# A two-layer attention and state-space kernel: ScalarE's table phases merged, loads reordered, B and C rows in four column tiles

## The chip, the cores and the metric

The kernel runs on one core of one Trainium2 chip. The metric is device time in microseconds of one launch; before the change the median of three runs is 849.88 us (849.84 to 852.37). A profile of one execution stands beside these runs. The engines are TensorE (PE; PEld are its weight loads), VectorE (DVE), ScalarE (ACT), GpSimd (POOL) and SyncE (SP), whose queue issues all DMAs here.

## The reference

Sixteen images of 16 x 16 positions and 64 channels go through two layers, all in float32.

- The first is attention over a 2 x 2 max-pooled image: `theta`, `phi` and `g` are projections of x, softmax of theta times phi weighs g, and the result, projected back, is added to x times `sigma`.
- The second reads each image in four directions (as it is, mirrored in width, in height, in both). Each direction is RMS-normalised and goes through a state-space mixer with 128 inner channels and 16 states: an input projection gives `hs` and `gate`; `hs` goes through a causal convolution of four taps and SiLU and becomes u; projections of u give a step width dt (through softplus) and, for every position, 16 values B and 16 values C. The recurrence is

```
state_n = exp(dt * A_n) * state_n + dt * B_n * u
y       = sum over n of state_n * C_n,  then  (y + u * D) * silu(gate),  projected back
```

The residual is added, RMS-normalised, the four directions are turned back and averaged, and a layer norm ends it.

## The kernel before

**Tiling.** 128 inner channels lie on the partitions, and the four directions of 256 positions stand side by side in 1024 columns. For each image and each of the 16 states n there is one scan of 128 x 1024 on VectorE (`scan`, L1129), with a decay factor and an input; where a direction begins, the step is overwritten with a huge number so that the decay is zero. The scanned state is multiplied with C's row (`product`), and TensorE adds the products of all states up in `ps_y` with an identity matmul (`sum_state`, L580).

**Three kinds of state.** The string `KIND = "ACCPACCCCPACPPCC"` says for each n who does what:

- C (1, 2, 5, 6, 7, 8, 11, 14, 15): ScalarE writes the decay into a PSUM tile `ps_x[n % 2]` (`ps_decay`, L798), POOL multiplies `du` with B's row (`scan_input`, L1000), VectorE scans inside `ps_x` and multiplies with C itself (L1146).
- P (3, 9, 12, 13): the same, but the scan goes to SBUF and POOL multiplies with C (L1008).
- A (0, 4, 10): ScalarE makes the input from transposed tiles, eight scalings each (`act_input`, L825), TensorE turns it into `ps_x` (`turn_input`, L564), the decay goes to SBUF (`sb_decay`, L806, called the shared decay in what follows), VectorE scans, POOL multiplies.

There are two tiles `ps_x`, so the decay of n may be written only when state n - 2 has let go of its tile: for kind C after its product, for the others after its scan (`x_free_wait`, L280). Decay 8 thus waits for product 6, decay 9 for product 7.

**Rows of B and C.** For an image, `bc_proj` (L491) projects u to 32 rows, ScalarE copies them to `bc_rows`, SP stores them to DRAM (`store_bc`), and loads them back row by row, each spread over 128 partitions (512 KB a load; `load_b`, L334, `load_c`, L341). B goes through a ring of four buffers that POOL's inputs release; C n waits for product n - 4. `bt_turn` (L545) transposes the rows for states of kind A.

**Order.** Every engine runs a list written out by hand: a prologue for the first two images, then `steps(b, done, coming, later)` for each image b, then a finish. In one step the engines work on four images: the scans of b, the end of the image before (`done`: gating, projection, norms), the preparation of the next (`coming`: norm, convolution, SiLU, softplus, rows), and the attention of the one after (`later`). Nothing is reordered at run time: an instruction that waits holds up what is behind it on its engine, and a load that waits holds up the loads behind it in SP's queue.

**ScalarE's tables.** SiLU, softplus and Exp/Ln belong to three table sets; `silu_table` (L772), `exp_table` (L775) and `softplus` (L784) load the set they need. In a step before the change the preparation of the next image has three phases, with decays of image b around them:

```
ps_decay 3 | pad, hid_inverse | silu_table, conv_silu half 0, exp_table | ps_decay 5
ps_decay 6 | silu_table, conv_silu half 1, gate_silu, exp_table | ps_decay 7
ps_decay 8 | softplus (own table), exp_table | ps_decay 9
```

The first half of the step projection (`step_proj`, L483) needs the gate copied out of its PSUM tile; softplus needs both halves. POOL's `scan_weight` (L991) follows softplus.

## Time and profile before

| | |
|---|---|
| median of the runs | 849.88 us (849.84 to 852.37) |
| profiled execution | 855.12 us |
| span of its instructions | 852.9 us |
| granted TensorE clock, mean | 0.988 |
| table loads on ScalarE | 94 (46 and 31 and 16, and one ahead) |
| DMA | 248.98 MB, mean 292 GB/s |

The span runs from the first to the last instruction of the profile; the execution's own time has a little around it. A row of a timeline gives the start in us from the span's start, the duration, engine, line, operation, what it writes and reads, and in brackets the engine's idle time before it and what ended it; like instructions that follow each other are merged ("x2"), so the row's duration is that of both. Instructions of an engine may overlap by a little, and matmuls in float32 appear as two records each. A row of the page's part 5 has the busy time of its group and the mean duration in ns.

### The profile page before, as it was taken

The page shows a single profiled execution, that of the slowest core. Times are in us where ns is not written, and L with a number is a line of the kernel's source. Part 1 is how long each engine was busy: PE and PEld are TensorE (multiplying, and loading weights), DVE is VectorE, ACT ScalarE, POOL GpSimd, SP SyncE. Part 2 cuts the span into 40 slices and gives each one's busy share as a digit, 9 for nine tenths or more (in the row PEclk, how much of TensorE's full clock was granted, in tenths as well). Part 3 has the DMA queues.
Part 4 walks back from the last instruction along what each step waited for, and adds up shares of the span by engine and source line. Part 5 has one row for each costly group of instructions (what it writes and reads, how often), then busy time and mean ns, then how long its engine had stood idle before and what let it go on. Part 6 is the DMA issues. An engine that isn't in the chain of part 4 may idle for free.

```text
span 852.9 us, 10113 instructions
## 1 busy us (share of the span) xinstructions
PE 792.3 (93%) x2592; PEld 386.7 (45%) x2592; DVE 787.9 (92%) x537; ACT 732.0 (86%) x1310; POOL 785.0 (92%) x363
## 2 busy tenths in 40 slices
PE   8489999999999999999999999999999999999795
PEld 6234444454444444444444544544454444444332
DVE  2299999999999999999999999999999999999992
ACT  5898989899898998989899998989999898987431
POOL 1399999999999999999999999999999999999980
PEclk9899999999999999999999999999999999999998
DMA  1679888889998989999898899988899988989870
GB/s 46 230 265 328 303 302 295 312 301 314 329 312 304 324 277 316 313 326 305 305 325 304 317 315 326 302 314 320 293 327 295 333 289 320 305 311 309 298 259 6
DMA packets 74472, 248.98 MB, mean 292 GB/s; under 512 B 12592, under 2 KB 13872, under 8 KB 74416
## 3 DMA queue, kind: packets, MB, share of 16 engines
q1 hardware_dynamic: 74416, 248.35, 85.0%
q8 instruction: 21, 0.34, 0.2%
q14 instruction: 35, 0.29, 0.1%
HBM read 245.17 MB, written 3.15 MB: 291 GB/s over the span
## 4 chain that ended last, share of the span: by engine, by line
POOL 40%; DMA 34%; issue 12%; PE 4%; DVE 3%; ACT 3%; SPq 3%; POOLq 0%; DVEq 0%; ACTq 0%
DMA b_all<-bc_dram 29%; POOL state L1011 19%; POOL inp L1005 18%; DMA c_all<-bc_dram 5%; POOL du L995 2%; SPq L344 2%; DVE state L1136 1%; PE ps_y L586 1%; DVE ps_x L1143 1%; ACT ps_x L804 1%; DVE state L1150 1%; PE ps_x L421 0%; ACT L786 0%; ACT L776 0%; ACT step L789 0%
## 5 line engine op out<-in xcount | busy, mean ns | idle before, releaser
L1005 POOL TENSOR_TENSOR inp<-du,b_all 128x1024 f32<-128x1024 f32 x208 | 487.7, 2364 | 14.5 <-issue 7.8
L586 PE MATMUL ps_y<-state,packed 128*128 128x512 f32 x1024 | 475.9, 600 | 17.6 <-POOL state L1011 16.9
L1143 DVE TENSOR_TENSOR_SCAN ps_x<-ps_x,inp 128x1024 f32<-128x1024 f32 x144 | 325.8, 2283 | 6.2 <-ACT ps_x L804 4.9
L586 PEld LDWEIGHTS ps_y<-state,packed 128*128 128x128 f32 x1024 | 188.2, 191 | 230.1 <-issue 183.5
L804 ACT ACTIVATE ps_x<-step,a_neg 128x1024 f32<-128x1024 f32 x208 | 231.0, 1111 | 48.5 <-DVE state L1150 21.8
L1011 POOL TENSOR_TENSOR state<-state,c_all 128x1024 f32<-128x1024 f32 x112 | 263.7, 2361 | 8.0 <-DVE state L1136 6.2
L1150 DVE TENSOR_TENSOR state<-ps_x,c_all 128x1024 f32<-128x1024 f32 x144 | 172.9, 1214 | 7.9 <-issue 3.9
L1143 DVE TENSOR_TENSOR_SCAN state<-ps_x,inp 128x1024 f32<-128x1024 f32 x64 | 145.7, 2279 | 3.1 <-issue 2.7
L1136 DVE TENSOR_TENSOR_SCAN state<-decay,ps_x 128x1024 f32<-128x1024 f32 x48 | 109.2, 2275 | 14.2 <-PE ps_x L572 12.8
L834 ACT ACTIVATE scaled<-dut,bt 128x128 f32<-128x128 f32 x384 | 117.1, 388 | 0.5
L475 PE MATMUL ps_w<-xpad,w_conv 128*128 128x512 f32 x128 | 60.4, 594 | 1.2 <-ACT xpad L762 1.2
L995 POOL TENSOR_TENSOR du<-step,u 128x1024 f32<-128x1024 f32 x16 | 37.9, 2370 | 24.0 <-ACT step L789 24.0
L776 ACT ACT_TABLE_LOAD x46 | 59.0, 1283 | 0.8
L572 PE MATMUL ps_x<-packed,scaled 128*128 128x128 f32 x384 | 51.4, 278 | 7.4 <-DVE state L1150 4.1
L572 PEld LDWEIGHTS ps_x<-packed,scaled 128*128 128x128 f32 x384 | 43.4, 142 | 28.6 <-issue 24.7
L811 ACT ACTIVATE decay<-step,a_neg 128x1024 f32<-128x1024 f32 x48 | 54.7, 1139 | 0.0
L773 ACT ACT_TABLE_LOAD x31 | 39.8, 1283 | 0.5
L475 PEld LDWEIGHTS ps_w<-xpad,w_conv 128*128 128x128 f32 x128 | 22.4, 188 | 33.9 <-issue 31.8
L577 PE MATMUL ps_y<-u,diag_d 128*128 128x512 f32 x64 | 34.2, 617 | 0.0
L488 PE MATMUL ps_w<-u,w_step 128*128 128x512 f32 x64 | 30.2, 594 | 0.0
L823 ACT ACTIVATE dut<-ps_w 128x512 f32<-128x512 f32 x32 | 19.1, 597 | 8.0 <-PE ps_w L561 7.2
L769 ACT ACTIVATE u<-ps_w,packed 128x512 f32<-128x512 f32 x32 | 21.9, 688 | 3.9 <-PE ps_w L475 3.6
(124 smaller groups left out, 642.4 us busy)
## 6 DMA issues: line engine op xcount, KB each, us to landing
c_all<-bc_dram SPq DMA_DIRECT2D x256, 512.0 KB, 6.2
b_all<-bc_dram SPq DMA_DIRECT2D x208, 512.0 KB, 6.6
bc_dram<-bc_rows SPq DMA_DIRECT2D x32, 64.0 KB, 2.2
xa<-in_x_t SPq DMA_DIRECT2D x16, 64.0 KB, 7.3
out<-ofin SPq DMA_DIRECT2D x16, 64.0 KB, 4.3
packed<-in_packed SPq DMA_DIRECT2D x1, 635.0 KB, 4.2
packed<-in_packed SPq DMA_DIRECT2D x1, 129.0 KB, 2.6
w_qkv<-in_w_qkv SPq DMA_DIRECT2D x1, 64.0 KB, 2.0
```

The source lines that it names most:

```text
L475: last = mm(ps_w[:, HALF * half:HALF * (half + 1)], w_conv[:, 2 * half + tap2, :], moved, start=(tap2 == 0), stop=(tap2 == 1))
L572: last = nc.tensor.transpose(ps_x[n % 2][:, 128 * k:128 * (k + 1)], scaled[i % A_RING][:, k, :], ident)
L586: last = mm(ps_y[:, HALF * half:HALF * (half + 1)], ident, state[n % H_RING][:, HALF * half:HALF * (half + 1)], start=(n == 0), stop=(n == ...
L776: act.preload_act_table_set(EXP_LN)
L804: f(ps_x[n % 2][:, :], step[b.buf][:, :], ACT.Exp, scale=a_neg[:, n:n + 1]).then_inc(ps_decay_done, 1)
L834: last = f(scaled[i % A_RING][:, k, :], dut[b.buf][:, k, :], ACT.Copy, scale=bt[b.buf][:, at, row:row + 1])
L995: tt(du[j.buf][:, :], step[j.buf][:, :], u[j.buf][:, :], ALU.mult).then_inc(du_done, 1)
L1005: tt(inp[i % IN_RING][:, :], du[b.buf][:, :], b_all[i % B_RING][:, :], ALU.mult).then_inc(pool_inputs, 1)
L1011: tt(state[n % H_RING][:, :], state[n % H_RING][:, :], c_all[n % C_RING][:, :], ALU.mult).then_inc(pool_products, 1)
L1136: v.tensor_tensor_scan(held, decay[i % D_RING][:, :], x, 0.0, ALU.mult, ALU.add).then_inc(scans, 1)
L1143: v.tensor_tensor_scan(held if KIND[n] == "P" else x, x, inp[i % IN_RING][:, :], 0.0, ALU.mult, ALU.add).then_inc(scans, 1)
L1150: v.tensor_tensor(state[n % H_RING][:, :], ps_x[n % 2][:, :], c_all[n % C_RING][:, :], ALU.mult).then_inc(dve_products, 1)
```

## The change

ScalarE: the second SiLU half, gate's SiLU and softplus follow each other between `ps_decay` 8 and 9, with one Exp load at their end; the first SiLU half moves behind `ps_decay` 6; `sb_decay` 10 moves ahead of `pad`, `sb_decay` 0 of the next image between decays 11 and 12; the residual of an image ends the step before. `bc_proj` makes its 32 rows for each direction (256 columns) in a column tile of its own, so that `bc_rows` is 128 x 256, is transposed in two pieces and stored in four. `hid_residual` is one matmul. SP loads B 6 and C 2 and 3 in the image before, and C 5 and 6 ahead of B 11; the next image's C 0 now stands ahead of its B 1. TensorE, VectorE and POOL have new orders; POOL does product 3 ahead of input 7. Warm-up multiplies are moved in the prologue and added in the finish. In the softmax the copy of `gw` follows the exponentials. The diff, cut to its core:

```diff
 SP, steps
-                load_b(b, 6)
-                load_c(b, 2)
-                load_c(b, 3)
-                load_c(b, 4)
                 load_b(b, 7)
                 load_b(b, 8)
                 load_b(b, 9)
-                load_b(b, 11)
+                load_c(b, 4)
                 load_c(b, 5)
                 load_c(b, 6)
+                load_b(b, 11)
                 load_b(b, 12)
...
                 load_c(b, 15)
                 if coming:
+                    load_c(coming, 0)
+                    load_b(coming, 1)
                     load_b(coming, 2)
+                    load_c(coming, 1)
                     load_b(coming, 3)
-                    load_c(coming, 0)
-                    load_c(coming, 1)
                     load_b(coming, 5)
+                    load_c(coming, 2)
+                    load_b(coming, 6)
+                    load_c(coming, 3)
 TensorE
-                for half in range(2):
-                    last = mm(bank[2 * N * half:2 * N * (half + 1), 0:HALF], w("w_bc"),
-                              u[j.buf][:, HALF * half:HALF * (half + 1)], start=True, stop=True)
+                for d in range(DIRS):
+                    last = mm(bank[2 * N * d:2 * N * (d + 1), 0:L], w("w_bc"), u[j.buf][:, L * d:L * (d + 1)],
+                              start=True, stop=True)
...
-                for rows in range(2):
-                    mm(w1[C * rows:C * (rows + 1), :], ident[:, C * rows:C * (rows + 1)],
-                       x2[j.num % X2_RING][:, :].unsqueeze(1).broadcast_to([128, 2, L]), start=True, stop=False)
+                mm(w1, ident, x2[j.num % X2_RING][:, :].unsqueeze(1).broadcast_to([128, 2, L]),
+                   start=True, stop=False)
 TensorE, finish
                 sum_state(j, 14)
-                hid_residual(j)
                 sum_state(j, 13)
                 sum_state(j, 15)
+                hid_residual(j)
                 hid_proj(j)
+                warm(2)
                 hid_mean(j)
+                warm(3)
                 out_mean(j)
+                warm(2)
                 out_square(j)
+                warm(2)
                 out_final(j)
 ScalarE, prologue
                 softplus(first)
                 exp_table(first)
+                softmax_exp(second)
                 bt_copy(first)
                 dut_copy(first, 0)
+                sb_decay(first, 0)
+                attn_copy(second)
                 dut_copy(first, 1)
                 act_input(first, 0)
-                sb_decay(first, 0)
+                residual(second)
                 act_input(first, 4)
 ScalarE, steps
+                ps_decay(b, 1)
                 sb_decay(b, 4)
                 if coming:
-                    residual(coming)
-                ps_decay(b, 1)
+                    rms_inverse(coming)
                 ps_decay(b, 2)
-                if coming:
-                    rms_inverse(coming)
+                ps_decay(b, 3)
                 act_input(b, 10)
                 if done:
                     hid_squares(done)
-                ps_decay(b, 3)
+                sb_decay(b, 10)
+                if done:
+                    hid_inverse(done)
                 if coming:
                     pad(coming)
-                if done:
-                    hid_inverse(done)
+                ps_decay(b, 5)
+                ps_decay(b, 6)
                 if coming:
                     silu_table(coming)
                     conv_silu(coming, 0)
                     exp_table(coming)
-                ps_decay(b, 5)
                 if done:
                     out_squares(done)
-                ps_decay(b, 6)
+                ps_decay(b, 7)
+                ps_decay(b, 8)
                 if coming:
                     silu_table(coming)
                     conv_silu(coming, 1)
                     gate_silu(coming)
-                    exp_table(coming)
-                ps_decay(b, 7)
-                sb_decay(b, 10)
-                ps_decay(b, 8)
-                if coming:
                     softplus(coming)
                     exp_table(coming)
                 ps_decay(b, 9)
                 if coming:
                     bc_copy(coming)
                     bt_copy(coming)
+                ps_decay(b, 11)
+                if coming:
                     dut_copy(coming, 0)
-                ps_decay(b, 11)
+                    sb_decay(coming, 0)
                 ps_decay(b, 12)
+                if coming:
+                    dut_copy(coming, 1)
                 if later:
                     theta_copy(later)
                 if coming:
-                    dut_copy(coming, 1)
                     act_input(coming, 0)
                 ps_decay(b, 13)
...
 POOL, steps
-                product(b, 3)
+                scan_input(b, 7)
                 scan_input(b, 8)
...
                     scan_input(coming, 6)
-                    scan_input(coming, 7)
+                    product(coming, 3)
 VectorE, steps
+                if done:
+                    product(done, 15)
                 scan(b, 0)
                 scan(b, 1)
+                if coming:
+                    rms(coming)
+                product(b, 1)
                 if done:
                     gated(done)
-                product(b, 1)
-                if coming:
-                    rms(coming)
                 scan(b, 2)
...
                 scan(b, 12)
+                scan(b, 13)
+                scan(b, 14)
+                if done:
+                    out_norm(done)
                 if later:
                     row_max(later)
-                scan(b, 13)
-                scan(b, 14)
-                if done:
-                    out_norm(done)
                 product(b, 14)
                 scan(b, 15)
-                product(b, 15)
```

## Rows read from the trace of the kernel before

**Rows 1.** The page, part 1: busy us, share of the span, instructions

```profile
PE 792.3 (93%) x2592; PEld 386.7 (45%) x2592; DVE 787.9 (92%) x537; ACT 732.0 (86%) x1310; POOL 785.0 (92%) x363
```

**Rows 2.** Timeline, DVE: start us, us; scan 10 of the first and last image

```profile
69.49 2.26 DVE L1136 TENSOR_TENSOR_SCAN state<-decay,ps_x 128x1024 f32<-128x1024 f32 x1
...
818.41 2.26 DVE L1136 TENSOR_TENSOR_SCAN state<-decay,ps_x 128x1024 f32<-128x1024 f32 x1
```

**Rows 3.** Timeline, DVE: scan 9, then scan 9 of the next image

```profile
616.10 2.29 DVE L1143 TENSOR_TENSOR_SCAN state<-ps_x,inp 128x1024 f32<-128x1024 f32 x1 [0.20 <-issue]
...
656.05 2.33 DVE L1150 TENSOR_TENSOR state<-ps_x,c_all 128x1024 f32<-128x1024 f32 x2
658.57 4.48 DVE L1143 TENSOR_TENSOR_SCAN ps_x<-ps_x,inp 128x1024 f32<-128x1024 f32 x2 [0.19 <-ACT ps_x L804]
662.96 2.33 DVE L1150 TENSOR_TENSOR state<-ps_x,c_all 128x1024 f32<-128x1024 f32 x2
665.49 2.29 DVE L1143 TENSOR_TENSOR_SCAN state<-ps_x,inp 128x1024 f32<-128x1024 f32 x1 [0.20 <-issue]
```

**Rows 4.** Timeline, ACT: the same stretch before that scan 9

```profile
654.44 0.69 ACT L769 ACTIVATE u<-ps_w,packed 128x512 f32<-128x512 f32 x1
655.03 0.65 ACT L782 ACTIVATE gate<-ps_w 128x256 f32<-128x256 f32 x2
...
658.40 1.13 ACT L811 ACTIVATE decay<-step,a_neg 128x1024 f32<-128x1024 f32 x1
659.44 1.10 ACT L804 ACTIVATE ps_x<-step,a_neg 128x1024 f32<-128x1024 f32 x1
660.56 1.28 ACT L786 ACT_TABLE_LOAD   x1
661.86 1.11 ACT L789 ACTIVATE step<-ps_w,packed 128x1024 f32<-128x1024 f32 x1
...
664.28 1.12 ACT L804 ACTIVATE ps_x<-step,a_neg 128x1024 f32<-128x1024 f32 x1
```

**Rows 5.** The page, part 5: one group of table loads

```profile
L773 ACT ACT_TABLE_LOAD x31 | 39.8, 1283 | 0.5
```

**Rows 6.** Timeline, PE: the step projection, both halves

```profile
655.79 1.88 PE L488 MATMUL ps_w<-u,w_step 128*128 128x512 f32 x4
```

**Rows 7.** Timeline, ACT: what stands ahead of the decay of scan 13

```profile
621.80 0.38 ACT L715 ACTIVATE theta<-ps_w 8x256 f32<-8x256 f32 x1
622.21 0.60 ACT L823 ACTIVATE dut<-ps_w 128x512 f32<-128x512 f32 x1
622.84 2.45 ACT L834 ACTIVATE scaled<-dut,bt 128x128 f32<-128x128 f32 x8
625.19 1.10 ACT L804 ACTIVATE ps_x<-step,a_neg 128x1024 f32<-128x1024 f32 x1
```

**Rows 8.** Timeline, DVE: the row maximum and scan 13

```profile
626.31 0.26 DVE L1118 TENSOR_REDUCE nmax<-ps_w 128x2 f32<-128x128 f32 x1
626.49 2.27 DVE L1143 TENSOR_TENSOR_SCAN state<-ps_x,inp 128x1024 f32<-128x1024 f32 x1
```

**Rows 9.** Timeline, POOL: product 12, then the next image's first input

```profile
626.46 2.35 POOL L1011 TENSOR_TENSOR state<-state,c_all 128x1024 f32<-128x1024 f32 x1 [0.20 <-DVE state L1143]
...
633.41 4.67 POOL L1005 TENSOR_TENSOR inp<-du,b_all 128x1024 f32<-128x1024 f32 x2
```

**Rows 10.** Timeline, SP's queue: a c load after product 12

```profile
628.88 0.32 SPq L344 DMA_DIRECT2D c_all<-bc_dram  x1
```

**Rows 11.** The page, part 6: DMA issues, KB each, median us to landing

```profile
b_all<-bc_dram SPq DMA_DIRECT2D x208, 512.0 KB, 6.6
```

**Rows 12.** Timeline, DVE: scan 1 of the first image

```profile
41.22 2.30 DVE L1143 TENSOR_TENSOR_SCAN ps_x<-ps_x,inp 128x1024 f32<-128x1024 f32 x1 [2.10 <-ACT ps_x L804]
```

**Rows 13.** Timeline, PE: the last image's residual multiply

```profile
834.09 1.08 PE L507 MATMUL ps_w<-x,packed 128*64 128x512 f32 x4
```

**Rows 14.** Timeline, DVE: the last image's gating

```profile
838.84 1.29 DVE L1161 TENSOR_TENSOR yg<-ps_y,gate 128x512 f32<-128x512 f32 x2 [3.25 <-PE ps_y L586]
```

More of the change, by code:

```diff
@@ L135, in build @@
         du = [sb(f"du_{q}", [I, T]) for q in range(2)]
-        bc_rows = sb("bc_rows", [128, HALF])
-        bt = [sb(f"bt_{q}", [128, HALF // 128, 4 * N]) for q in range(2)]
+        bc_rows = sb("bc_rows", [128, L])
+        bt = [sb(f"bt_{q}", [128, CHUNKS, 2 * N * DIRS]) for q in range(2)]
         dut = [sb(f"dut_{q}", [128, TURNS, I]) for q in range(2)]
@@ L357, in prologue @@
                 load_b(first, 2)
+                load_c(first, 0)
                 load_b(first, 3)
-                load_c(first, 0)
                 load_c(first, 1)
                 load_b(first, 5)
+                load_c(first, 2)
+                load_b(first, 6)
+                load_c(first, 3)
             def finish(j):
@@ L496, in bc_proj @@
                 bank = ps_w if j.num > 0 else ps_y
-                for half in range(2):
-                    last = mm(bank[2 * N * half:2 * N * (half + 1), 0:HALF], w("w_bc"),
-                              u[j.buf][:, HALF * half:HALF * (half + 1)], start=True, stop=True)
+                for d in range(DIRS):
+                    last = mm(bank[2 * N * d:2 * N * (d + 1), 0:L], w("w_bc"), u[j.buf][:, L * d:L * (d + 1)],
+                              start=True, stop=True)
                 last.then_inc(bc_mm, 1)
@@ L548, in bt_turn @@
                 if j.num == 0:
-                    pe.wait_ge(rows_zeroed, 1)
                     pe.wait_ge(step_done, 1)
-                for k in range(HALF // 128):
+                for k in range(CHUNKS):
                     last = nc.tensor.transpose(w0[:, 128 * k:128 * (k + 1)], bc_rows[:, 128 * k:128 * (k + 1)], ident)
@@ L614, in prologue @@
                 conv(first, 1)
-                attn_turn(second)
                 pe.wait_ge(weights_ready, 1)
@@ L831, in act_input @@
                 for k in range(TURNS):
-                    half, at = k // (TURNS // 2), k % (TURNS // 2)
-                    row = 2 * N * half + n
+                    at = k % CHUNKS
+                    row = 2 * N * (k // CHUNKS) + n
                     last = f(scaled[i % A_RING][:, k, :], dut[b.buf][:, k, :], ACT.Copy,
@@ L886, in prologue @@
                 pad(first)
-                softmax_exp(second)
+                state_decay()
                 silu_table(first)
@@ L1017, in prologue @@
                 scan_input(first, 1)
+                scan_input(first, 2)
                 product(first, 0)
-                scan_input(first, 2)
                 scan_input(first, 3)
@@ L1022, in prologue @@
                 scan_input(first, 6)
-                scan_input(first, 7)
+                product(first, 3)
             def finish(j):
@@ L1180, in prologue @@
                 pooling(first)
+                attn_setup()
                 row_max(first)
-                attn_setup()
+                rms(first)
+                pooling(second)
                 conv_setup()
                 setup()
-                rms(first)
-                pooling(second)
+                first_bc(first)
                 row_max(second)
-                first_bc(first)
             def finish(j):
+                product(j, 15)
                 gated(j)
@@ L1223, in steps @@
                 scan(b, 12)
-                if later:
-                    row_max(later)
                 scan(b, 13)
```

91 lines of the change are left out of this document (43 added, 48 removed).

## The prediction

> **What bounds the kernel now.** I read the busy shares first: TensorE, VectorE and POOL are each busy for 92 or 93% of the span, ScalarE for 86% [rows 1]. Such a share is a mean over prologue, images and tail, so I then followed VectorE's timeline, because its scans are a strict series: scan 9 of one image starts at 616.10 and of the next at 665.49, a period of 49.39 us [rows 3]. VectorE's 787.9 us over 16 images is 49.2 per image [rows 1]. **VectorE has next to no air in a period**, and POOL, with 785.0, only a little more. A wait that VectorE gains in each image is therefore paid in full, 15 or 16 times.
>
> The whole of it: scan 10 of the first image starts at 69.49 and of the last at 818.41, so 15 periods take 748.92 [rows 2]. Fifteen times 49.39 is 740.85; 8.07 us are lost in longer periods. The profiled execution took 855.12 and the median of the runs is 849.88, 5.24 lower, so I suppose that 2.8 of those 8.07 are left in the median run. Without them the profiled execution would take 847.05; call this the floor of the old order.
>
> In each period there is one place that the change touches and where ScalarE already ends a wait of VectorE. Product 6 ends at 658.38 and scan 9 starts at 665.49, 7.11 us later, after scans 7 and 8 and products 7 and 8; there VectorE idles 0.20 us [rows 3]. ScalarE's rows say why: the decay that scan 9 reads starts at 664.28, directly behind softplus and the load of the Exp table, and ends 0.09 before the scan [rows 4]. Nothing can be put ahead of this decay without moving scan 9.
>
> **The one large term: the merged phase.** Before, the second SiLU half and gate's SiLU ran between decays 6 and 7 with a phase of their own. Now they stand between decay 8 and softplus; the shared decay of state 10 leaves its place between decays 7 and 8. Decay 8 overwrites the PSUM tile that product 6 has read, so it starts 0.1 behind product 6 at the earliest (the hand-over in the other direction is 0.09). From there, by [rows 4] with the table load of [rows 5]: decay 8 takes 1.12 until the next starts; SiLU table 1.28; second SiLU half 0.59; gate's SiLU 0.65; softplus table 1.30; softplus and Exp table together 2.42; decay 9 with its hand-over 1.21. With the 0.1 that is 8.67 after product 6, against VectorE's 7.11: scan 9 starts **1.56 us later in every image that has a next one, 15 times: 23.4 us**. As a lower end I take 1.2, both hand-overs free and ScalarE's instructions overlapping by some 0.1 [rows 7]; a gain is excluded, since decay 8 cannot start before product 6 ends and the chain has no gap. For the upper end: softplus needs both halves of the step projection, and the first half needs the gate copied out. Two halves take 1.88 on TensorE [rows 6]; the second runs beside the gate's SiLU, the first ends 663.35 on the old clock, 0.07 before softplus could start. If both had to follow the gate, softplus would be 0.6 later: 2.2 per image.
>
> One table load less per image shortens ScalarE by 15 x 1.28 = 19 us of its 732 [rows 1, 5]. I cost this at nothing: what it shortens is the stretch from decay 3 to decay 7, and decay 7 waits for product 5 there. Into that stretch go the shared decay of state 10 (1.04, [rows 4]) and the padding ahead of decay 5; if the load's 1.28 less did not cover them, scan 5 would be late by what is left over, which I take as none.
>
> **A second, small wait.** The shared decay of state 0 moves from behind decay 15 to between decays 11 and 12. From the start of scan 9, the chain to scan 13 is then: scan 9 2.29, hand-over 0.1, decay 11 1.12, first transposed copy 0.63, the shared decay 1.04, decay 12 1.12, second copy 0.63, theta 0.41, eight scalings 2.35, decay 13 1.10, hand-over 0.09: 10.88 [rows 3, 4, 7]. VectorE's own way is 626.49 - 616.10 less 0.18 for the row maximum, which moves behind scan 14: 10.21 [rows 3, 8]. The wait is between nothing and 0.67. Where two such instructions follow each other the second starts some 0.1 early (1.13 long, 1.04 apart); with that for the decays and copies it is 0.27, which I take: 15 x 0.27 = **4.1 us**.
>
> **SP's order and the narrower rows.** Loads of B 6 and C 2 and 3 move into the image before, C 5 goes ahead of B 11, and four row stores replace two. An issue takes 0.32 [rows 10]; two more per image lie behind C 12's load, and the loads behind them wait for later products anyway. I cost that at nothing. Its cover is the new, longer period; without it, see the second rival. Earlier C loads and longer periods should end the 8.07 of loss; I take all of it as gone, ends 0 and 8.07. Four column tiles and half the transposes take only TensorE time: two tiles side by side do four records in 1.08, where one tile needs 1.88 [rows 6, 13]. The residual in one matmul is so worth some 0.14, the B and C rows between nothing and half of 1.08. TensorE waits for products between these; nothing. On VectorE, the row scaling and product 1 now precede the gating; nothing is added or removed.
>
> **Head.** Residual of the second image and the first decay now run ahead of where VectorE waited 2.10 us for decay 1 [rows 12]; softmax moves behind softplus, the first product after one more B row. I take -2.1, between nothing and -4, since the first scan itself may come earlier. **Tail.** The last gating waited 3.25 us for the sums, of which 1.08 were the residual multiply ahead of them; this now runs behind them, beside the gating: -1.1 [rows 13, 14]. Warm-up multiplies fill TensorE's waits there; as nine calls of a quarter of that width, two records each, they would cost 2.4 us at most if nothing hid them.
>
> **The sum**, on the profiled execution: 855.12 - 8.07 + 23.4 + 4.1 - 2.1 - 1.1 = 871.4 us. From the median, with its 2.8 of loss taken off, it is the same. That the forecast and this sum agree with the unprofiled time rests on the supposition that the 5.24 are such loss; if none of it goes, the time is 874 by the median, 879 by the profile.
>
> **Rivals.** *Faster: less table loading reaches the end.* If VectorE had room for the late decay 9, what stays is the floor without head and tail gains paid back: 847.05 - 3.2 = 843.9, or 846.7 with the loss kept. It decides if the merged phase fits into 7.11 us after product 6, which needs 1.56 us less on ScalarE, more than one whole load. For it speaks that ScalarE is the least busy of the four [rows 1]; against it, that scan 9 waits already. Chance 0.11. The Trainium skill (page "ScalarE: Activation LUTs", section "Rules for kernel authors") has this as a rule: group functions by table set and finish one set before switching, which speaks for the change. The same page (section "What ACT_TABLE_LOAD costs") counts a drain beside a load, 2.66 us per switch; by this an estimated 40 us of ScalarE would be saved, and the one switch that now comes between products would make scan 9 a further 1.38 us later. The load's 1283 ns agree with this trace; a drain behind it does not show, as softplus starts 0.02 behind its load [rows 4, 5].
>
> *POOL becomes the bound.* The next image's first B load now queues behind its C 0 load, and that waits for product 12. Product 12 ends at 628.81; the C issue starts 0.07 later and takes 0.32 [rows 9, 10], and a B load lands 6.6 us after its own issue [rows 11]: 635.9 with the gap between issues, where POOL wanted it at 633.41. POOL's cycle, 785.0/16 = 49.1, would be 51.6 and VectorE's 49.39 + 1.83 = 51.2: 15 x 0.4 = 6 more, 877. It decides once a landing takes over 6.3; at 8 it gives 897. Chance 0.13. Early loads and an emptier queue speak against it.
>
> **How the numbers follow.** The forecast has 0.76; its own range is 861 (1.2 per image, no second wait) to 883 (0.6 more per image, some loss kept). The range 858 to 883 holds that, most of the second rival, and leaves the faster one out. About 0.3% is what a measurement here can tell from no change, 847.3 to 852.4. The faster rival lies mostly below: 0.08 faster, 0.03 same; the rest, 0.89, slower.
>
> **What would show it.** Right: periods of about 51.2 between scans 9; ScalarE's new row group in a series SiLU load, SiLU, gate, softplus load, softplus, Exp load; VectorE's wait before scan 9 near 1.8, released by a decay; 15 table loads fewer. Wrong: no such wait, or periods near 49.4 (first rival), or POOL idle over 2 us before its first input with VectorE waiting for that input (second).

## The result and the profile after

The changed kernel takes 866.82 us (median of four runs, 865.56 to 868.55), the kernel before beside it 851.12 (849.84 to 853.27): a ratio of **1.0169, 95% interval 1.0141 to 1.0198**. It is 15.7 us slower. The forecast was 871.4 with a range of 858 to 883. The profiled execution took 868.55 with a span of 866.5 and a mean granted clock of 0.973; before it was 855.12, 852.9 and 0.988.

The page after the change, part 1 (busy us, share of the span, instructions), as [rows 1]:

```profile
PE 790.1 (91%) x2610; PEld 389.2 (45%) x2610; DVE 783.0 (90%) x537; ACT 710.2 (82%) x1295; POOL 784.8 (91%) x362
```

ScalarE has 15 instructions fewer and is busy for 21.8 us less than the 732.0 before; VectorE (787.9 before) and POOL (785.0) have nearly the work that they had. The engine that was relieved was not the one that sets the period. The timeline of VectorE after, scan 10 of the first and of the last image, as [rows 2]:

```profile
70.02 2.26 DVE L1136 TENSOR_TENSOR_SCAN state<-decay,ps_x 128x1024 f32<-128x1024 f32 x1
...
834.12 2.26 DVE L1136 TENSOR_TENSOR_SCAN state<-decay,ps_x 128x1024 f32<-128x1024 f32 x1
```

So the head takes 70.02 us (69.49 before), the 15 periods 764.10 (748.92 before), and what follows the last of these scans 866.5 - 834.12 = 32.4 (34.5 before). The loss lies in the periods. Here is one of them on VectorE, from scan 9 to scan 9 of the next image, as [rows 3]:

```profile
628.27 2.29 DVE L1143 TENSOR_TENSOR_SCAN state<-ps_x,inp 128x1024 f32<-128x1024 f32 x1 [2.02 <-issue]
...
667.98 2.33 DVE L1150 TENSOR_TENSOR state<-ps_x,c_all 128x1024 f32<-128x1024 f32 x2
670.50 4.48 DVE L1143 TENSOR_TENSOR_SCAN ps_x<-ps_x,inp 128x1024 f32<-128x1024 f32 x2 [0.19 <-ACT ps_x L807]
674.89 2.33 DVE L1150 TENSOR_TENSOR state<-ps_x,c_all 128x1024 f32<-128x1024 f32 x2
679.24 2.29 DVE L1143 TENSOR_TENSOR_SCAN state<-ps_x,inp 128x1024 f32<-128x1024 f32 x1 [2.01 <-issue]
```

The period is 679.24 - 628.27 = 50.97 us, against 49.39. Cut it at products 5 and 6. From scan 9 to their start: 39.71 now, 656.05 - 616.10 = 39.95 before. From there to the next scan 9: 11.26 now, 665.49 - 656.05 = 9.44 before. **The whole loss, 1.82 us, lies between product 6 and scan 9**, and the rest of the period has become 0.24 shorter. The page's part 5 shows the same wait over the whole run (busy us, mean ns, idle time before and what ended most of it), with two groups of table loads beside it:

```profile
L1143 DVE TENSOR_TENSOR_SCAN state<-ps_x,inp 128x1024 f32<-128x1024 f32 x64 | 146.0, 2282 | 32.2 <-issue 30.4
...
L776 ACT ACT_TABLE_LOAD x31 | 39.8, 1283 | 0.5
L779 ACT ACT_TABLE_LOAD x31 | 39.8, 1283 | 0.5
```

30.4 us over 15 images are 2.03 each. With softplus's own 16 and the one ahead there are 79 table loads, 15 fewer than the 94 before. What VectorE waits for stands in ScalarE's timeline of the same stretch, as [rows 4]; it begins with decays 7 and 8:

```profile
669.28 2.25 ACT L807 ACTIVATE ps_x<-step,a_neg 128x1024 f32<-128x1024 f32 x2 [0.41 <-DVE state L1150]
671.54 1.28 ACT L776 ACT_TABLE_LOAD   x1
672.84 0.69 ACT L772 ACTIVATE u<-ps_w,packed 128x512 f32<-128x512 f32 x1
673.42 0.65 ACT L785 ACTIVATE gate<-ps_w 128x256 f32<-128x256 f32 x2
674.09 1.28 ACT L789 ACT_TABLE_LOAD   x1
675.60 1.11 ACT L792 ACTIVATE step<-ps_w,packed 128x1024 f32<-128x1024 f32 x1 [0.23 <-PE ps_w L489]
676.73 1.28 ACT L779 ACT_TABLE_LOAD   x1
678.03 1.12 ACT L807 ACTIVATE ps_x<-step,a_neg 128x1024 f32<-128x1024 f32 x1
```

This is the forecast's chain, in its order: SiLU load, second SiLU half, gate's SiLU, softplus load, softplus, Exp load, decay 9. The decay ends at 679.15, 0.09 before scan 9. There is one gap in it, 0.23 us, in which softplus waits for TensorE's step projection (line 489). That row of TensorE, as [rows 6]:

```profile
673.58 1.98 PE L489 MATMUL ps_w<-u,w_step 128*128 128x512 f32 x4 [0.89 <-ACT u L772]
```

All four of its records start behind the second SiLU half and end at 675.56, when the softplus table had been in place for 0.19 us.

### The profile page after: what moved, and what is told of

Its sections match the earlier page's. It is cut to its first block, busy times and chain, and to the rows that moved or that the text cites. A ratio compares the mean times of both kernels' runs of the same rounds, so it can differ in the third digit from the quotient of the medians.

```text
span 866.5 us, 10149 instructions
## 1 busy us (share of the span) xinstructions
PE 790.1 (91%) x2610; PEld 389.2 (45%) x2610; DVE 783.0 (90%) x537; ACT 710.2 (82%) x1295; POOL 784.8 (91%) x362
## 4 chain that ended last, share of the span: by engine, by line
DMA 22%; DVE 18%; ACT 15%; issue 13%; POOL 11%; PE 9%; SPq 1%; DVEq 0%; ACTq 0%; POOLq 0%
DMA b_all<-bc_dram 14%; DMA c_all<-bc_dram 8%; DVE state L1143 7%; POOL inp L1006 7%; DVE ps_x L1143 5%; PE ps_y L585 5%; ACT ps_x L807 5%; ACT scaled L837 4%; DVE state L1150 4%; POOL state L1012 4%; ACT L776 2%; ACT dut L826 2%; PE ps_w L476 1%; DVE state L1136 1%; ACT u L772 1%
## 5 line engine op out<-in xcount | busy, mean ns | idle before, releaser
L1006 POOL TENSOR_TENSOR inp<-du,b_all 128x1024 f32<-128x1024 f32 x208 | 486.3, 2359 | 19.6 <-issue 13.1
L585 PEld LDWEIGHTS ps_y<-state,packed 128*128 128x128 f32 x1024 | 190.4, 192 | 207.7 <-issue 189.8
L1143 DVE TENSOR_TENSOR_SCAN state<-ps_x,inp 128x1024 f32<-128x1024 f32 x64 | 146.0, 2282 | 32.2 <-issue 30.4
L1136 DVE TENSOR_TENSOR_SCAN state<-decay,ps_x 128x1024 f32<-128x1024 f32 x48 | 109.1, 2272 | 12.7 <-PE ps_x L571 12.7
L476 PE MATMUL ps_w<-xpad,w_conv 128*128 128x512 f32 x128 | 63.0, 616 | 9.4 <-ACT ocen L861 9.4
L776 ACT ACT_TABLE_LOAD x31 | 39.8, 1283 | 0.5
L779 ACT ACT_TABLE_LOAD x31 | 39.8, 1283 | 0.5
L515 PE MATMUL ps_w<-yg,packed 128*64 128x256 f32 x128 | 20.0, 405 | 9.9 <-DVE yg L1161 9.9
```

The lines of the kernel that those rows point to most:

```text
L476: last = mm(ps_w[:, HALF * half:HALF * (half + 1)], w_conv[:, 2 * half + tap2, :], moved, start=(tap2 == 0), stop=(tap2 == 1))
L585: last = mm(ps_y[:, HALF * half:HALF * (half + 1)], ident, state[n % H_RING][:, HALF * half:HALF * (half + 1)], start=(n == 0), stop=(n == ...
L776: act.preload_act_table_set(SILU)
L1006: tt(inp[i % IN_RING][:, :], du[b.buf][:, :], b_all[i % B_RING][:, :], ALU.mult).then_inc(pool_inputs, 1)
L1136: v.tensor_tensor_scan(held, decay[i % D_RING][:, :], x, 0.0, ALU.mult, ALU.add).then_inc(scans, 1)
L1143: v.tensor_tensor_scan(held if KIND[n] == "P" else x, x, inp[i % IN_RING][:, :], 0.0, ALU.mult, ALU.add).then_inc(scans, 1)
```

## Experiments

Two theories stood at the start. **Mine:** VectorE's series of scans sets the period, and whatever ScalarE does between decay 8 and decay 9 is paid in full, because decay 8 waits for product 6 and scan 9 for decay 9. **The rival:** the new order of SP's queue (C 0 ahead of B 1) or the new orders of the other engines cost the time, and the merged phase is innocent. The ratios below are to the kernel before, run beside each experiment.

**1. The merged phase alone, in the kernel before.** Decay 10 goes to the vacated place, and the step projection behind sum 4:

```diff
 ScalarE, steps
                 ps_decay(b, 6)
+                sb_decay(b, 10)
+                ps_decay(b, 7)
+                ps_decay(b, 8)
                 if coming:
...
                     gate_silu(coming)
-                    exp_table(coming)
-                ps_decay(b, 7)
-                sb_decay(b, 10)
-                ps_decay(b, 8)
-                if coming:
                     softplus(coming)
 TensorE, steps
                 sum_state(b, 3)
+                sum_state(b, 4)
                 if coming:
...
                     step_proj(coming, 0)
-                sum_state(b, 4)
```

> The kernel before with the merged phase alone: second SiLU half and gate's SiLU move from between decays 6 and 7 to between decay 8 and softplus, one Exp load per image goes, decay 10 of the shared kind takes the vacated place, TensorE's step projection follows sum 4. Loads, rows, head and tail as before. Theory (VectorE pays for a late decay 9): VectorE waits about 2.0 us before scan 9 in 15 images instead of 0.2, the period is 51.0 to 51.3, the time 868 to 876. Rival (the loss comes from SP's order or from POOL, the merged phase is free): period 49.4 to 50, time 843 to 852.

Measured: 905.96 us (903.60 to 910.43), ratio 1.0632 (1.0591 to 1.0673), far above what was expected. VectorE's timeline of one image:

```profile
609.70 2.29 DVE L1141 TENSOR_TENSOR_SCAN state<-ps_x,inp 128x1024 f32<-128x1024 f32 x1 [2.01 <-issue]
612.42 2.29 DVE L1134 TENSOR_TENSOR_SCAN state<-decay,ps_x 128x1024 f32<-128x1024 f32 x1 [0.42 <-PE ps_x L572]
615.00 2.30 DVE L1141 TENSOR_TENSOR_SCAN ps_x<-ps_x,inp 128x1024 f32<-128x1024 f32 x1 [0.29 <-ACT ps_x L804]
```

and the step projection in TensorE's, just ahead of it:

```profile
604.05 1.98 PE L488 MATMUL ps_w<-u,w_step 128*128 128x512 f32 x4 [2.29 <-ACT u L769]
```

The wait before scan 9 is there, and over the run it is longer than in the changed kernel: 44.8 us in 16 waits, where the changed kernel has 30.4 in 15. But the old order of TensorE has the sums and B and C's projection behind the step projection and ahead of the turned input of state 10 (line 572); all of it is held up for 2.29 us, and scans 10 and 11 wait too. So the merged phase has a price by itself, and in the old order a higher one. That the changed kernel's order of TensorE, with its sums spread between, keeps it near 1.8 us is my reading; that order was not tried alone.

**2. The reverse: three phases again in the changed kernel.** ScalarE from the inputs of state 10 to decay 9, and TensorE from sum 1 to sum 4, get their old order; all else stays:

```diff
 ScalarE, steps
...
+                    exp_table(coming)
+                ps_decay(b, 7)
+                sb_decay(b, 10)
+                ps_decay(b, 8)
+                if coming:
                     softplus(coming)
 TensorE, steps
-                turn_input(b, 4)
                 sum_state(b, 1)
-                sum_state(b, 2)
                 if coming:
                     conv(coming, 0)
+                turn_input(b, 4)
...
```

> The changed kernel with ScalarE's stretch from act_input 10 to decay 9 and TensorE's from sum 1 to sum 4 as they were before, so three phases and one Exp load more per image; all else as changed. Theory: the wait before scan 9 falls back to 0.2; the period falls from 50.97 to between 49.4 (VectorE sets it) and 49.85 (POOL sets it, with its wait for the next image's B 1, which now stands behind C 0); time 843 to 851. Rival (the loss is not in the merged phase): 864 to 870, as the changed kernel.

Measured: 895.49 us (894.94 to 895.90), ratio 1.0502 (1.0481 to 1.0524): a miss. VectorE's timeline has the wait before scan 9 back at 0.20, and two others in its place:

```profile
633.87 2.29 DVE L1139 TENSOR_TENSOR_SCAN state<-decay,ps_x 128x1024 f32<-128x1024 f32 x1 [1.58 <-PE ps_x L571]
...
662.92 2.29 DVE L1146 TENSOR_TENSOR_SCAN state<-ps_x,inp 128x1024 f32<-128x1024 f32 x1 [1.96 <-ACT ps_x L808]
```

Scan 4 waits for a turned input that now stands behind a convolution, scan 13 for a late decay. Each half of the old order fits the old rest alone. The two experiments show that the phases cannot be judged in a mixture of orders; the next ones change one thing inside a whole order.

**3. One SiLU load more on the chain, one Exp load more beside it.** Each adds 15 loads of 1.28 us; only the place differs. The first attempt at the former put two SiLU loads directly behind each other:

```diff
                 if coming:
                     silu_table(coming)
+                    silu_table(coming)
                     conv_silu(coming, 1)
```

> The changed kernel with the SiLU table loaded twice in the merged phase, 15 loads of 1.28 us more. Theory: every us put between decay 8 and decay 9 is paid in full: the wait before scan 9 is 3.3 us, the period 52.25, the time 886 (866.8 + 19.2). Rival (VectorE has room left there): under 875.

Measured: 865.75 us (864.21 to 867.10), ratio 1.0148 (1.0121 to 1.0174). It says nothing of the theory: the page still counts 31 loads on line 776, so the second was not there to be paid. The second attempt puts it behind the second SiLU half:

```diff
                     conv_silu(coming, 1)
+                    silu_table(coming)
                     gate_silu(coming)
```

> The changed kernel with the SiLU table loaded once more inside the merged phase, between the second SiLU half and gate's SiLU (two loads right behind each other left only one in the run before). Theory: each us between decay 8 and decay 9 is paid in full, so the wait before scan 9 is 3.3 us instead of 2.03, the period 52.2, the time 884 to 888. Rival (VectorE has room there): under 872.

```diff
                     bt_copy(coming)
+                    exp_table(coming)
                 ps_decay(b, 11)
```

> The changed kernel with one more load of the Exp table per image, ahead of decay 11, where ScalarE waits 1.26 us for scan 9: the same 15 loads of 1.28 us, at another place. Theory (only the place counts): time within 2 us of the changed kernel's 866.8. Rival (ScalarE's load counts wherever it stands): 886.

On the chain: 888.12 us (median of three runs, 886.56 to 889.32; a fourth took 1146.5 at a mean granted clock of 0.65, where the three had 0.97, and is not counted), ratio 1.0400 (1.0337 to 1.0463), 21.3 us above the changed kernel. Beside the chain: 866.11 us (865.24 to 867.01), ratio 1.0158 (1.0137 to 1.0180), no difference. The page's part 5, first the kernel with the load on the chain:

```profile
L1144 DVE TENSOR_TENSOR_SCAN state<-ps_x,inp 128x1024 f32<-128x1024 f32 x64 | 146.0, 2282 | 53.5 <-issue 51.8
...
L776 ACT ACT_TABLE_LOAD x46 | 59.0, 1283 | 0.8
```

then the kernel with the load beside it:

```profile
L1144 DVE TENSOR_TENSOR_SCAN state<-ps_x,inp 128x1024 f32<-128x1024 f32 x64 | 146.0, 2283 | 32.9 <-issue 32.7
...
L779 ACT ACT_TABLE_LOAD x46 | 59.0, 1283 | 0.8
```

Both have 46 loads in a group where there were 31. In one, VectorE's wait grew from 30.4 to 51.8 us, by 21.4; in the other it is what it was. **The place of a table load decides, not the number of loads.** This carries the theory, and it also shows why saving 15 loads elsewhere bought nothing.

**4. The SiLU load taken off the chain.** From the second image on the second half goes through Identity and gate through Copy, so their SiLU is left out. The instructions keep their lengths, 0.67 and 0.65 us where they took 0.69 and 0.65:

```diff
-                    silu_table(coming)
                     conv_silu(coming, 1)
-                    gate_silu(coming)
+                    gate_silu(coming, ACT.Copy)
```

> The changed kernel with the SiLU load of the merged phase taken out: from the second image on, the second half and the gate go through identity and copy instead of SiLU, so that part of the computation is left out; durations of the instructions stay. Theory: the wait before scan 9 falls by 1.28 to about 0.75, the period to 49.7 unless POOL (48.9 of work and about 0.95 of wait for B 1) keeps it at 49.85; time 847 to 851. Rival (another engine sets the period near 51): 860 or more.

Measured: 854.17 us (851.60 to 854.94), ratio 1.0011 (0.9989 to 1.0033). Nearly all of the loss is gone, though 3 us less than I expected. What is left shows in one image's scan 9 on VectorE and, in the second fence, in ScalarE's rows ahead of it:

```profile
670.15 2.29 DVE L1143 TENSOR_TENSOR_SCAN state<-ps_x,inp 128x1024 f32<-128x1024 f32 x1 [1.46 <-POOL inp L1006]
```

```profile
666.52 1.11 ACT L793 ACTIVATE step<-ps_w,packed 128x1024 f32<-128x1024 f32 x1 [1.07 <-PE ps_w L489]
...
668.94 1.12 ACT L808 ACTIVATE ps_x<-step,a_neg 128x1024 f32<-128x1024 f32 x1
```

The page names POOL's input as what ended the wait; it is a case for reading twice. The decay ends at 668.94 + 1.12 = 670.06, again 0.09 before the scan, and POOL's row for that input, which ends at 669.67, ends earlier. ScalarE is still last, now because softplus waits 1.07 us for the step projection where it waited 0.23: of the 1.28 us taken away, 0.84 became a longer wait for TensorE. TensorE has a sum ahead of the step projection here, and this sum waited for a product of POOL:

```profile
662.78 1.98 PE L585 MATMUL ps_y<-state,packed 128*128 128x512 f32 x4 [0.34 <-POOL state L1012]
```

**5. All orders of ScalarE, TensorE and VectorE as before, in prologue and steps; SP's and POOL's orders, the column tiles, the row stores and the finish as changed.** The core of the edit:

```diff
 ScalarE, steps
...
                     gate_silu(coming)
+                    exp_table(coming)
+                ps_decay(b, 7)
+                sb_decay(b, 10)
+                ps_decay(b, 8)
+                if coming:
                     softplus(coming)
 TensorE, steps
...
                     step_proj(coming, 0)
+                sum_state(b, 4)
                 sum_state(b, 5)
+                sum_state(b, 6)
                 if coming:
                     bc_proj(coming)
...
```

> The changed kernel with the orders of ScalarE, TensorE and VectorE (prologue and steps) as before, hence three phases as before; SP's and POOL's orders, the column tiles, the single residual matmul and the finish stay as changed. Theory: no wait of 2 us before scan 9; period 49.4 (VectorE) to 49.85 (POOL, whose first input of an image waits for B 1 behind C 0); the tail keeps its 2 us: 843 to 851. Rival (SP's and POOL's orders or the rows cost by themselves): 856 or more.

Measured: 856.14 us (853.68 to 859.77), ratio 1.0038 (1.0016 to 1.0060): 10.7 below the changed kernel, but not the 843 to 851 I expected. VectorE's wait before scan 9 is gone (its group idles 2.9 us in all). What is left is on POOL, in the page's part 5:

```profile
L1007 POOL TENSOR_TENSOR inp<-du,b_all 128x1024 f32<-128x1024 f32 x208 | 486.5, 2360 | 19.8 <-DVE ps_x L1144 9.9
```

The releaser named there ended 11 waits, 9.9 us in all; where one image follows another, the one that waits is POOL's first input of the next image. The second rival has a mechanism for them: B 1's load queues on SP behind C 0's, which waits for product 12. The page names VectorE as the releaser; whether it is the load, the next two runs tell, which move that one load, here and in the changed kernel.

**6. B 1 issued ahead of C 0**, first in the kernel of experiment 5, then in the changed kernel:

```diff
 SP, steps
                 load_c(b, 15)
                 if coming:
-                    load_c(coming, 0)
                     load_b(coming, 1)
+                    load_c(coming, 0)
                     load_b(coming, 2)
```

> The run with the orders put back (three phases), with one more edit on SP: the next image's B 1 is issued behind C 15 and ahead of C 0 instead of behind it, so that it no longer waits for product 12. Theory: POOL's wait before the first input of an image, which set the period of 50.1 there, goes; VectorE sets the period again, 49.4 to 49.7; time 844 to 849, under the kernel before. Rival (the lost time is in the four row stores or in product 3 ahead of input 7): 853 or more.

> The changed kernel with B 1 issued ahead of C 0, nothing else. Theory: POOL's wait for B 1 goes, but VectorE's wait before scan 9 sets the period there, so the time stays: 864 to 868. Rival (POOL shares in the 50.97): 860 or less.

With the old orders: **844.71 us (843.79 to 846.91), ratio 0.9920 (0.9889 to 0.9951)**, faster than both kernels. In the changed kernel: 864.29 us (863.98 to 865.02), ratio 1.0141 (1.0107 to 1.0176), 2.5 us below it, with overlapping intervals. POOL's group of the first kernel, with VectorE's scan 9 in two successive images:

```profile
L1007 POOL TENSOR_TENSOR inp<-du,b_all 128x1024 f32<-128x1024 f32 x208 | 487.0, 2364 | 3.8 <-DMA b_all<-bc_dram 2.9
```

```profile
610.44 2.29 DVE L1144 TENSOR_TENSOR_SCAN state<-ps_x,inp 128x1024 f32<-128x1024 f32 x1 [0.20 <-issue]
...
659.90 2.29 DVE L1144 TENSOR_TENSOR_SCAN state<-ps_x,inp 128x1024 f32<-128x1024 f32 x1 [0.20 <-issue]
```

and the page's part 5 of the second:

```profile
L1006 POOL TENSOR_TENSOR inp<-du,b_all 128x1024 f32<-128x1024 f32 x208 | 486.5, 2359 | 3.6 <-DMA b_all<-bc_dram 2.7
...
L1143 DVE TENSOR_TENSOR_SCAN state<-ps_x,inp 128x1024 f32<-128x1024 f32 x64 | 146.0, 2282 | 32.0 <-issue 30.1
```

POOL's idle time falls by 16 us in both (from 19.8 and, in the changed kernel, 19.6). In the one the period falls to 659.90 - 610.44 = 49.46; in the other VectorE's wait is as long as ever. B 1's late load is real in the changed kernel, and hidden there behind VectorE's wait; with that wait gone it is what binds. The two kernels of this experiment differ only in the orders of ScalarE, TensorE and VectorE, so those orders cost 864.29 - 844.71 = 19.6 us. TensorE's granted clock does not explain it: its mean is 0.985 in the profiled execution of the first and 0.982 in that of the second.

**7. Two phases: both SiLU halves and gate in one, between decays 6 and 7, softplus alone.** TensorE's turned input of state 4, convolutions and gate projection change places to suit, and B 1 stands ahead of C 13 in the first kernel, ahead of C 0 in the second; the rest is as in experiment 5. ScalarE's edit:

```diff
 ScalarE, steps
-                if coming:
-                    silu_table(coming)
-                    conv_silu(coming, 0)
-                    exp_table(coming)
                 ps_decay(b, 5)
...
                     silu_table(coming)
+                    conv_silu(coming, 0)
                     conv_silu(coming, 1)
                     gate_silu(coming)
```

> As the run with the orders put back, but with two phases at the other place: both SiLU halves and gate's SiLU between decays 6 and 7 with one Exp load, softplus alone between decays 8 and 9; TensorE's turn of state 4 ahead of the first convolution half, the gate's projection behind the second; and B 1 of the next image loaded ahead of C 13 again. Two loads per image fewer than before. Theory: the phase of 4.5 us fits between decays 6 and 7, nothing is added between 8 and 9: waits before scans 4, 5 and 9 at most 0.2, period 49.1 to 49.5, time 840 to 848. Rival (fewer loads do not matter, a stall of TensorE's order comes in their place): 850 or more.

> The run with two phases (both SiLU halves and the gate between decays 6 and 7), with B 1 behind C 15 and ahead of C 0 instead of ahead of C 13, where it held C 13 to 15 back until the rows were stored. Theory: products no longer wait for C rows; waits before scans 4 and 5 stay gone, about 0.6 before scan 7 stays: period 49.3 to 49.8, time 843 to 850. Rival (TensorE's order has stalls of its own): 855 or more.

The first: 868.56 us (865.43 to 871.79), ratio 1.0173 (1.0126 to 1.0221), a miss. VectorE's waits show why (line that waits, us in total, times, longest):

```profile
DVE state L1148 <- issue: 22.5, 13, 2.8
```

SP's waits have the other end of it (line 337 issues the loads of B):

```profile
SPq L337 <- DMA bc_dram<-bc_rows: 93.6, 16, 7.5
```

VectorE's products (line 1148) wait 13 times, for C rows; a B 1 that stands ahead of C 13 must wait for the row stores, and holds C 13 to 15 back behind it. The second, with B 1 two places later: 845.99 us (844.70 to 848.26), ratio 0.9931 (0.9907 to 0.9955), as expected. It has 30 table loads fewer than the kernel of experiment 6 that took 844.71 (15 fewer than the changed one), ScalarE is busy for 690.8 us instead of 726.4, and it is no faster.

**8. Column tiles, narrow rows, four stores and the single residual alone, in the kernel before.**

```diff
-                for half in range(2):
-                    last = mm(bank[2 * N * half:2 * N * (half + 1), 0:HALF], w("w_bc"),
-                              u[j.buf][:, HALF * half:HALF * (half + 1)], start=True, stop=True)
+                for d in range(DIRS):
+                    last = mm(bank[2 * N * d:2 * N * (d + 1), 0:L], w("w_bc"), u[j.buf][:, L * d:L * (d + 1)],
+                              start=True, stop=True)
...
```

> The kernel before with the narrower rows and the single residual matmul alone: four column tiles for B and C, 128 x 256 rows, two transposes instead of four, four stores of 32 KB instead of two of 64 KB, one residual matmul; all orders and loads as before. Theory (costed at nothing, since TensorE waits between these): within 0.3% of the kernel before, 848 to 854. Rival (four stores land later and hold the loads behind them): 856 or more; or (TensorE's shorter work comes through): under 847.

Measured: 850.92 us (846.76 to 854.15) against 852.29, ratio 0.9979 (0.9959 to 1.0000). This half of the change is worth nothing that can be told, as costed.

## Why the prediction was right, and where its terms were off

The sign, the mechanism and the place were right, and the likeliest case came. On the profiled execution the sum said +16.3 us and the trace shows +13.4. That it came so near owes something to luck, since its errors have both signs: about +3.9 us in the merged phase, -7.7 around the second wait, +1.4 in the old loss, +0.8 in the head and -1.0 in the tail. On the medians the forecast was +21.5, from 849.88 to 871.4, and +15.7 came. The 5.24 between the two forecasts are the supposition that the median run lacked part of the old loss; no run shows that, as only profiled executions have a trace. Step by step:

- **The merged phase, 1.56 us per image: 1.82 measured, the right term and too small.** The working held down to single rows, but I set the step projection at nothing: it was to be ready "0.07 before softplus could start". That counted its 1.88 from 0.59 behind the start of the second SiLU half. In the trace this SiLU ends 0.69 behind its start, the projection starts 0.05 behind that end and takes 1.98, and softplus starts 0.04 behind the projection: it waits 0.23. With it the term is 1.79. A margin of 0.07 was none, where rows overlap by 0.1; the upper end of 2.2 had such a wait in it. (The 7.11 us from product 6 to scan 9 also hold a wait of 0.19 before scan 7, which "there VectorE idles 0.20 us" leaves out; it is there after the change too and alters nothing.) Experiments 3 and 4 show that the term is what binds: +1.28 us on the chain cost 21.3 us, -1.28 gave back 12.7.
- **The second wait, 0.27 at scan 13: some 0.2 came, and more than that went elsewhere.** The stretch from scan 9 to products 5 and 6 became 0.24 shorter where the sum has it 0.27 longer; 15 x 0.51 = 7.7 us is the largest error of the sum. VectorE's timeline has it in two pieces; scans 14, 4 and 5 before:

```profile
628.68 2.26 DVE L1143 TENSOR_TENSOR_SCAN ps_x<-ps_x,inp 128x1024 f32<-128x1024 f32 x1
...
649.31 2.29 DVE L1136 TENSOR_TENSOR_SCAN state<-decay,ps_x 128x1024 f32<-128x1024 f32 x1
651.66 4.48 DVE L1143 TENSOR_TENSOR_SCAN ps_x<-ps_x,inp 128x1024 f32<-128x1024 f32 x2
```

  and after:

```profile
640.88 2.27 DVE L1143 TENSOR_TENSOR_SCAN ps_x<-ps_x,inp 128x1024 f32<-128x1024 f32 x1
...
661.42 2.28 DVE L1136 TENSOR_TENSOR_SCAN state<-decay,ps_x 128x1024 f32<-128x1024 f32 x1
663.62 4.45 DVE L1143 TENSOR_TENSOR_SCAN ps_x<-ps_x,inp 128x1024 f32<-128x1024 f32 x2
```

  From scan 9 to scan 14 it is 12.61 us now and was 12.58, although the row maximum (0.18) has left this piece: a wait of 0.21 came. From scan 14 to products 5 and 6 it is 27.10 and was 27.37, although the row maximum has come in: some 0.45 of waits has gone. They were too small for the timeline to mark. One shows in the fences: scan 5 started 2.35 behind scan 4 and starts 2.20 behind it now. I had asked what the new orders add there and not what they take away.
- **The 8.07 us of loss in longer periods, taken as gone: right to 1.4.** Fourteen periods with the wait and one without would take 15 x (50.97 - 1.82) + 14 x 1.82 = 762.7; they took 764.10. Experiment 6 shows the loss gone without any help from a longer period: in its first kernel scan 10 starts at 67.93 in the first image and at 809.37 in the last, 15 periods of 49.43. ScalarE, TensorE and VectorE have their old orders there, and the rows are worth nothing (experiment 8); what is left, besides a copy in the softmax, are the new orders of SP, with B 1 moved, and of POOL, which were not tried apart. The change thus contained a gain, and covered it with a larger loss.
- **Head, -2.1: the wait went, but the first scan came later.** Scan 1 now follows scan 0 at once instead of waiting 2.10 as in [rows 12], but scan 0 itself starts 1.06 later than before, at 37.89 instead of 36.83. TensorE's granted clock is part of that. VectorE's first scans after:

```profile
37.89 2.29 DVE L1136 TENSOR_TENSOR_SCAN state<-decay,ps_x 128x1024 f32<-128x1024 f32 x1 [12.68 <-PE ps_x L571]
40.09 2.27 DVE L1143 TENSOR_TENSOR_SCAN ps_x<-ps_x,inp 128x1024 f32<-128x1024 f32 x1
```

  TensorE's first convolutions in the same execution, and the stretch from 15 to 20 us (us, busy time and count of PE, PEld, DVE, ACT and POOL, granted clock, DMA share, GB/s):

```profile
17.56 5.54 PE L476 MATMUL ps_w<-xpad,w_conv 128*128 128x512 f32 x8
```

```profile
15.00:20.00 5.00, 4.76 (x12) 2.89 (x12) 2.96 (x14) 3.43 (x7) 0.00 (x0) 0.50 0.00 0
```

  The second kernel of experiment 6 has the same prologue, and there the clock had risen:

```profile
17.73 3.67 PE L476 MATMUL ps_w<-xpad,w_conv 128*128 128x512 f32 x8 [0.66 <-ACT xpad L765]
```

```profile
15.00:20.00 5.00, 3.90 (x16) 2.28 (x15) 2.96 (x14) 3.70 (x8) 0.00 (x0) 0.97 0.00 0
```

  Its scan 0 starts at 36.19, 1.70 earlier. The order is another part: the first kernel of experiment 6 has the old prologue of ScalarE, TensorE and VectorE and nearly the same clock, 0.99 in that stretch, and its scan 0 starts 1.02 ahead of this:

```profile
35.17 2.29 DVE L1137 TENSOR_TENSOR_SCAN state<-decay,ps_x 128x1024 f32<-128x1024 f32 x1 [12.80 <-PE ps_x L571]
```

  Scan 1 starts at 39.55 there and at 38.39 in the second kernel, so in this pair the new head is worth 1.2 us, not 2.1. I had asked only if the first scan might come earlier. The figure is rough: in the traces kept, scan 0 starts anywhere from 35.08 to 36.83 with the old prologue and from 36.19 to 37.89 with the new one.
- **Tail, -1.1: -2.1.** The last gating waits 2.08 us instead of the 3.25 of [rows 14], the 1.1 of the residual. I gave the added warm-up multiplies only a cost; the last two products of TensorE became shorter, from 1.19 to 0.67 us and from 1.12 to 0.66.
- **The first rival, less table loading reaches the end, fell.** Fifteen loads more beside the chain cost nothing (experiment 3), and 30 fewer bought nothing (experiment 7). The rule of the Trainium skill (page "ScalarE: Activation LUTs", section "Rules for kernel authors"), to finish one table set before switching, saved 15 loads, and each load takes the 1283 ns of the page's section "What ACT_TABLE_LOAD costs". The drain that this section adds does not show: where nothing else is waited for, the instruction after a load starts 0.01 or 0.02 us behind it. No run here shows a gain from the rule; following it put one load more onto the chain that binds.
- **The second rival, B 1 behind C 0, was real and not the bound.** POOL idled some 1 us an image for it, not over 2; moved ahead it was worth 2.5 us at most while VectorE waits, and 11.4 (856.14 to 844.71) where it doesn't.

What stays open: the run of 1146.5 us in experiment 3, what SP's order and POOL's are worth apart, and which of the moved instructions of ScalarE or TensorE took each of the small waits away, which was not tried one by one.

## What to carry to other kernels

Before phases are merged to save table loads, write down between which two waits the merged phase will stand: a load saved on an engine with air was worth nothing here, and a load moved between a release and the instruction that the busiest engine waits for was paid in every round. Where a change mixes reorderings, split it by engine and by queue: here the orders of SP and POOL held a gain that showed only after the phases had been put back and one load moved two lines. And when a wait is removed, look for what is late next, in the timeline and not only in the name that the page gives the releaser.

## What the runs showed of the hardware

- **Two equal table loads directly behind each other leave one in the trace** (experiment 3: 31 on line 776 as without the second). With a SiLU between them both stand there, 46.
- **The granted clock in the prologue differs between executions of the same instructions**: 0.50 or 0.97 in the stretch from 15 to 20 us, and with it 5.54 or 3.67 us for the same convolutions.
- **After two waits in the middle of an image the clock stood at its lower level, 1.2 GHz.** In experiment 2 TensorE idles 2.02 us and, one group of 0.64 us later, 1.68; the next sums take 3.31 us where 1.88 is usual (from TensorE's timeline; then the stretch in its windows, columns as above):

```profile
647.67 0.64 PE L499 MATMUL ps_w<-u,packed 128*32 128x256 f32 x8 [2.02 <-ACT step L793]
649.99 1.94 PE L571 MATMUL ps_x<-packed,scaled 128*128 128x128 f32 x8 [1.68 <-DVE state L1153]
...
652.15 3.31 PE L585 MATMUL ps_y<-state,packed 128*128 128x512 f32 x4
```

```profile
650.00:655.00 5.00, 5.00 (x14) 3.40 (x15) 4.96 (x3) 1.65 (x3) 4.92 (x4) 0.50 0.94 236
```

  In experiment 1 it idles 1.43 and 2.29 us with 1.98 us of sums between, and there the clock stays at 1.00.

- **A small store's landing is not set by its size.** In the old queue the four stores of 32 KB land 2.0 us after their issue (experiment 8, the page's part 6), about as the two of 64 KB in the kernel before, 2.2; in the changed kernel they take 4.5 (the same part; KB each, median us to landing):

```profile
bc_dram<-bc_rows SPq DMA_DIRECT2D x64, 32.0 KB, 4.5
```

  With the same queue it is 3.0 in experiment 3, with the load on the chain, and 6.0 in experiment 4, so the order of the queue alone does not set it either; what does was not tried.
